# A recommendation model's last tile: layer 4 with features on partitions, an output layer as two products, sums in quarters, and the other tiles' logits stored ahead

## The reference

```
fm = emb_table[arange(26)[None, :], cat_idx]                 # 26 rows of 128
dense = relu(relu(relu(x @ Wd1 + bd1) @ Wd2 + bd2) @ Wdf + bdf)
Z = concatenate([fm, dense[:, None, :]], axis=1)
interactions = einsum('bie,bje->bij', Z, Z)[:, iu, ju]       # 351 pairs
x = concatenate([interactions, dense], axis=-1)
x = relu(x @ Wt1 + bt1); x = relu(x @ Wt2 + bt2)
x = relu(x @ Wt3 + bt3); x = relu(x @ Wt4 + bt4)             # 512 -> 256 in Wt4
return sigmoid(x @ Wo + bo)
```

## Time and profile before

| | us |
|---|---|
| median of 3 runs | 176.47 (176.35 to 177.85) |
| profiled execution | 176.1 |
| its span, first to last instruction | 174.3 |
| TensorE busy | 161.2 (93%) |
| VectorE busy | 72.2 (41%) |
| ScalarE busy | 62.4 (36%) |
| GpSimd busy | 99.9 (57%) |

### The profile page before, as it was taken

The page is one execution under the profiler, slowest core; times in us unless marked ns, Lnnn a source line. Parts: engine busy times, 40 slices in busy tenths (PEclk is TensorE's granted clock), DMA queues, the critical chain, the costliest instruction groups (busy, mean ns, idle before and its releaser), DMA issues.

```text
span 174.3 us, 3885 instructions
## 1 busy us (share of the span) xinstructions
PE 161.2 (93%) x1691; PEld 115.7 (66%) x1691; DVE 72.2 (41%) x139; ACT 62.4 (36%) x108; POOL 99.9 (57%) x111
## 2 busy tenths in 40 slices
PE   2999999589999998899999999999999999999983
PEld 1334464345768785678787867877877777788971
DVE  5005276786664662553504225163212453411311
ACT  3377597848476772031211121311111230201110
POOL 4777777777777777777777777777775000000000
PEclk9999999999999999999999999999999999999999
DMA  2999999329855422121212121211222000000000
GB/s 60 331 385 264 240 315 342 137 58 310 314 171 175 146 56 52 47 64 45 60 49 58 51 56 54 54 52 50 59 49 60 4 0 0 0 4 0 0 0 0
DMA packets 6674, 18.18 MB, mean 104 GB/s; under 512 B 2309, under 2 KB 2441, under 8 KB 6530
## 3 DMA queue, kind: packets, MB, share of 16 engines
q1 hardware_dynamic: 3330, 11.12, 19.6%
q0 software_dynamic: 3328, 6.82, 14.4%
HBM read 17.93 MB, written 0.00 MB: 103 GB/s over the span
## 4 chain that ended last, share of the span: by engine, by line
PE 59%; POOL 21%; issue 8%; DMA 6%; ACT 2%; DVE 1%; DVEq 0%
PE mp L484 23%; POOL rows L345 21%; PE mp L451 8%; PE mp L507 7%; DMA rows<-in_emb,row_of 5%; PE gp L410 4%; PE gp L400 4%; PE tp L459 4%; PE gp L525 3%; PE tp L548 3%; PE mp L548 1%; DMA idx<-in_cat_idx 1%; ACT zt L634 1%; ACT xth L646 1%; ACT a2h L654 1%
## 5 line engine op out<-in xcount | busy, mean ns | idle before, releaser
L345 POOL DMA_INDIRECT rows<-in_emb,row_of x104 | 99.0, 952 | 33.1 <-issue 28.9
L484 PE MATMUL mp<-w2l,a1h 128*128 128x512 f32 x64 | 26.8, 418 | 0.0
L484 PE MATMUL mp<-w2h,a1h 128*128 128x512 f32 x64 | 26.2, 410 | 0.0
L484 PE MATMUL mp<-w2h,a1l 128*128 128x512 f32 x64 | 25.5, 399 | 0.0
L634 ACT COPY zt<-gp 128x512 f32<-128x512 f32 x16 | 9.4, 586 | 31.4 <-PE gp L400 31.3
L400 PE MATMUL gp<-ident,rows 128*128 128x128 f32 x104 | 16.7, 275 | 3.6 <-DMA rows<-in_emb,row_of 3.5
L400 PEld LDWEIGHTS gp<-ident,rows 128*128 128x128 f32 x104 | 12.7, 140 | 10.0 <-DMA rows<-in_emb,row_of 5.8
L410 PEld LDWEIGHTS gp<-zt 128*32 128x32 f32 x1024 | 11.2, 110 | 8.2 <-issue 6.8
L814 DVE TENSOR_TENSOR raw<-mp,bc 128x512 f32<-128x512 f32 x8 | 5.5, 691 | 25.6 <-PE mp L484 25.6
L410 PE MATMUL gp<-zt 128*32 128x27 f32 x1024 | 13.3, 195 | 1.3 <-DVE zt L785 0.8
L484 PEld LDWEIGHTS mp<-w2h,a1l 128*128 128x128 f32 x64 | 12.1, 189 | 2.9 <-DVE a1l L808 0.9
(11 more groups left out here) (85 smaller groups left out, 246.2 us busy)
## 6 DMA issues: line engine op xcount, KB each, us to landing
w<-in_wt SPq DMA_DIRECT2D x13, 512.0 KB, 5.0
rows<-in_emb,row_of POOLq DMA_INDIRECT x104, 2.8
w<-in_wt SPq DMA_DIRECT2D x3, 468.0 KB
bc<-in_rows SPq DMA_DIRECT2D x1, 1024.0 KB, 6.2
wd_sb<-in_wd SPq DMA_DIRECT2D x1, 512.0 KB, 3.5
w1d<-in_wt SPq DMA_DIRECT2D x1, 512.0 KB, 6.1
bt<-in_rows SPq DMA_DIRECT2D x1, 512.0 KB, 8.6
wdf_sb<-in_wdf SPq DMA_DIRECT2D x1, 128.0 KB, 3.3
```

The lines of the kernel that those rows point to most:

```text
L345: pool.indirect_dma_start(out=rows[:, n % RING, :], out_offset=None, in_=emb.rearrange("c v e -> (c v) e"), in_offset=bass.IndirectOffsetO ...
L484: last = pe.matmul(sums_of(t, 2 + h), a[:, k, :], w[:, k, cols], start=(k == 0 and part == 0), stop=(k == M1 - 1 and part == 2))
```

## The change

It touches the fourth tile's last layers and the output.

- The small constants in `sm` get four more columns: the two halves of `bt4` and the two of `Wo`, one value for each partition.
- The second half of layer 3's sum is added in two quarters of 128 columns, each transposed by itself, and each with its own relu. `last_turn` now does one transpose.
- `last_layer_4` takes 128 columns of `w4[:, k]` as the weights in the array and streams `a3[:, k, :]`, for two halves m of the output features: eight products of 128 columns, and the result has output features on partitions, in `mp[:, 0]` and `mp[:, 1]`.
- Bias and relu of half 0 are one instruction of ScalarE, of half 1 one of VectorE, each with a bias per partition, into `a4`.
- The output layer of this tile is two products with a column of `Wo` as the weights (one column wide) and `a4[:, m, :]` streamed; the result is one row of 128 logits.
- The logits of the first three tiles are transposed between layer 2 and layer 3 of the fourth tile, get their sigmoid there, and are stored with a transfer of their own. The fourth tile's row has its own sigmoid and transfer. SP waits for both at the end.

```diff
-for _name, _n in (("bd1", 4), ("bd2", 2), ("bdf", 1), ("bo", 1)):
+for _name, _n in (("bd1", 4), ("bd2", 2), ("bdf", 1), ("bo", 1), ("bt4", 2), ("Wo", 2)):
...
             sp.wait_ge(probs_ready, 1)
-            sp.dma_start(out.rearrange("(t p) c -> t (p c)", p=P), probs[:]).then_inc(out_done, 16)
-            sp.wait_ge(out_done, 16)
+            sp.dma_start(rows_out[0:TILES - 1, :], probs[:]).then_inc(out_done, 16)
+            sp.wait_ge(probs_ready, 2)
+            sp.dma_start(rows_out[TILES - 1:TILES, :], last_probs[:]).then_inc(out_done, 16)
+            sp.wait_ge(out_done, 32)
...
+            def last_turn(t, k):
+
+                pe.wait_ge(raw_ready, TURNS * t + 4 + (1 if k < 2 else k))
+                pe.transpose(last_turned(k, k + 1), raw[:, 0, k * P:(k + 1) * P], ident[:]).then_inc(turned, 1)
...
+            def last_layer_4(t):
+
+                for k in range(M3):
+                    pe.wait_ge(a3_ready, t + (1 if k < 2 else k))
+                    for m in range(2):
+                        last = pe.matmul(mp[:, m, 0:P], w4[:, k, m * P:(m + 1) * P], a3[:, k, :], start=(k == 0), stop=(k == M3 - 1))
+                        if k == M3 - 1:
+                            last.then_inc(l4_ready, 1)
+                        if k < 2 and m == 1 - k:
+                            last_turn(t, 2 + k)
+
+            def turn_logits():
+
+                pe.wait_ge(logits_ready, TILES - 1)
+                pe.transpose(gp[:, 0, 0:P], logits[:], ident[:]).then_inc(logits_turned, 1)
+
+            def last_logits():
+
+                for m in range(2):
+                    pe.wait_ge(a4_act if m == 0 else a4_dve, 1)
+                    last = pe.matmul(gp[0:1, 1, 0:P], sm[:, COLS["Wo"] + m:COLS["Wo"] + m + 1], a4[:, m, :], start=(m == 0), stop=(m == 1))
+                last.then_inc(logits_turned, 1)
...
             layer_1(t)
             layer_2(t)
+            turn_logits()
             last_layer_3(t)
-            layer_4(t)
-            pe.wait_ge(logits_ready, TILES)
-            pe.transpose(mp[:, 0, 0:P], logits[:], ident[:]).then_inc(logits_turned, 1)
+            last_layer_4(t)
+            last_logits()
...
             layer_2_hi(t, 0)
+            sigmoid()
             layer_2_hi(t, 1)
-            for h in range(2):
-                sc.wait_ge(turned, TURNS * t + 4 + h + 1)
-                sc.activation(a3[:, 2 * h:2 * h + 2, :].rearrange("p m b -> p (m b)"), tp[:, h, 0:2 * P], ACT.Relu).then_inc(a3_ready, 1)
-            sigmoid()
+            for k0, k1 in ((0, 2), (2, 3), (3, 4)):
+                sc.wait_ge(turned, TURNS * t + 4 + k1)
+                sc.activation(a3[:, k0:k1, :].rearrange("p m b -> p (m b)"), last_turned(k0, k1), ACT.Relu).then_inc(a3_ready, 1)
+            sc.wait_ge(l4_ready, t + 1)
+            sc.activation(a4[:, 0, :], mp[:, 0, 0:P], ACT.Relu, bias=bias("bt4", 0)).then_inc(a4_act, 1)
+            last_sigmoid()
...
-            for h in range(2):
-                ve.wait_ge(l3_ready, t + h + 1)
-                ve.tensor_tensor(raw[:, 0, 2 * h * P:2 * (h + 1) * P], gp[:, 2 + h, 0:TOP[3] // 2],
-                                 bc[:, ROW3 + 2 * h * P:ROW3 + 2 * (h + 1) * P], ALU.add).then_inc(raw_ready, 1)
-            last_layers(t)
+            for k0, k1 in ((0, 2), (2, 3), (3, 4)):
+                ve.wait_ge(l3_ready, t + k0 // 2 + 1)
+                ve.tensor_tensor(raw[:, 0, k0 * P:k1 * P], gp[:, 2 + k0 // 2, (k0 % 2) * P:((k1 - 1) % 2 + 1) * P],
+                                 bc[:, ROW3 + k0 * P:ROW3 + k1 * P], ALU.add).then_inc(raw_ready, 1)
+            ve.wait_ge(l4_ready, t + 2)
+            ve.tensor_scalar(a4[:, 1, :], mp[:, 1, 0:P], bias("bt4", 1), 0.0, ALU.add, ALU.max).then_inc(a4_dve, 1)
```

More of the change, by code:

```diff
@@ L156, in build @@
         logits = sb("logits", [P, P])
-        probs = sb("probs", [TILES, P])
+        probs = sb("probs", [TILES - 1, P])
+        last_probs = sb("last_probs", [1, P])
+        a4 = sb("a4", [P, 2, P])
         table_warm = sb("table_warm", [P, 1])
@@ L227, in build @@
         a3_ready = sem("a3_ready")
+        a4_act = sem("a4_act")
+        a4_dve = sem("a4_dve")
         l4_ready = sem("l4_ready")
@@ L240, in sums_of, with last_turned @@
             return mp[:, (SUMS * t + i) % 2, :]
-        def layer_4_sums(t):
-            return (tp if t < TILES - 1 else mp)[:, 1, 0:TOP[4]]
+        def last_turned(k0, k1):
+            return tp[:, 1, 0:P] if k0 == 2 else tp[:, 0, (k0 % 3) * P:(k0 % 3 + k1 - k0) * P]
         def pairs_by_chunk(c0, c1):
@@ L323, in _ @@
             sp.dma_start(w4[:].rearrange("p k n -> p (k n)"), wt4).then_inc(w4_in, 16)
+            rows_out = out.rearrange("(t p) c -> t (p c)", p=P)
             sp.wait_ge(probs_ready, 1)
-            sp.dma_start(out.rearrange("(t p) c -> t (p c)", p=P), probs[:]).then_inc(out_done, 16)
-            sp.wait_ge(out_done, 16)
+            sp.dma_start(rows_out[0:TILES - 1, :], probs[:]).then_inc(out_done, 16)
+            sp.wait_ge(probs_ready, 2)
+            sp.dma_start(rows_out[TILES - 1:TILES, :], last_probs[:]).then_inc(out_done, 16)
+            sp.wait_ge(out_done, 32)
         @block.gpsimd
@@ L518, in last_layer_3 @@
                                 last_turn(t, 0)
+                                last_turn(t, 1)
                             k, part = 4 * half + n // 3, n % 3
@@ L541, in layer_4 @@
                 for k in range(M3):
-                    if t < TILES - 1 and k == 0:
+                    if k == 0:
                         pe.wait_ge(a3_ready, t + 1)
[L544 to L548, removed]
-                last.then_inc(l4_ready, 1)
+                    last = pe.matmul(tp[:, 1, 0:TOP[4]], a3[:, k, :], w4[:, k, :], start=(k == 0), stop=(k == M3 - 1))
+                last.then_inc(l4_ready, 1)
+            def last_layer_4(t):
[15 more added lines that the diff above has]
+                last.then_inc(logits_turned, 1)
             def keep_warm(n):
@@ L661, in sigmoid, with last_sigmoid @@
                 sc.wait_ge(logits_turned, 1)
-                sc.activation(probs[:], mp[0:TILES, 0, 0:P], ACT.Sigmoid, bias=sm[0:TILES, COLS["bo"]:COLS["bo"] + 1]).then_inc(probs_ready, 1)
+                sc.activation(probs[:], gp[0:TILES - 1, 0, 0:P], ACT.Sigmoid, bias=sm[0:TILES - 1, COLS["bo"]:COLS["bo"] + 1]).then_inc(probs_ready, 1)
+            def last_sigmoid():
+                sc.wait_ge(logits_turned, 2)
+                sc.activation(last_probs[:], gp[0:1, 1, 0:P], ACT.Sigmoid, bias=sm[0:1, COLS["bo"]:COLS["bo"] + 1]).then_inc(probs_ready, 1)
             sc.wait_ge(ident_made, 2)
@@ L829, in last_layers @@
                 ve.wait_ge(l4_ready, t + 1)
-                ve.tensor_tensor(z4[:, 0, :], layer_4_sums(t), bc[:, ROW4:ROW4 + TOP[4]], ALU.add).then_inc(z4_ready, 1)
+                ve.tensor_tensor(z4[:, 0, :], tp[:, 1, 0:TOP[4]], bc[:, ROW4:ROW4 + TOP[4]], ALU.add).then_inc(z4_ready, 1)
                 ve.wait_ge(z4_ready, t + 1)
```

## The result

| | before | after |
|---|---|---|
| median | 176.66 us (12 runs, 176.30 to 177.85) | 175.37 us (12 runs, 175.09 to 176.14) |
| profiled execution | 176.1 us | 175.6 us |
| its span | 174.3 us | 173.8 us |

The ratio is 0.9926, with a 95% interval of 0.9908 to 0.9944: 1.3 us faster, between 1.0 and 1.6. The forecast was a gain of 1.0 us and a time of 175.5 us.

A forecast was written before the change was run, and what follows sets the result against it. TensorE gapless to 168.15 us, then a 4.56 us chain of short dependent instructions to the store. Its steps, including +0.11 and -0.62 us, moved the store from 172.71 to 171.70: 176.47 - 1.0 = 175.5 us, range 174.9 to 176.5.

The forecast's parts named there:

- relay: Short dependent instructions from the last layer 3 product's end to the last store's issue; 4.56 us before the change.
- Step 1: Three tiles' logits transposed between layers 2 and 3 of the last tile: +0.11 us, with the early sigmoid hidden.
- tail: From the last store's issue to the span's end: taken as unchanged at 1.59 us.
- rival of a much shorter tail: After the last store's issue: most of 0.9 us of waiting vanishes, sum near -1.8 us, 174.7 us; chance 0.05.
- Step 2: Second half of layer 3's sum on VectorE: each quarter 0.29 us instead of 0.42 us for the whole half.
- Step 3: Layer 4 as 16 passes of 128 columns at 0.11 us: ends at 170.38 instead of 171.00, -0.62 us.
- bounds: In layer 4: if waits expose loads at k = 2 or k = 3, up to 0.2 us less gain.
- Steps 4 to 6: Behind layer 4: relus (VectorE 0.40 us, ending last), output products, sigmoid; store at 171.70 instead of 172.71.
- Trainium skill's rule against step 3: In layer 4: weight loads overlap products only in other array rows, so 16 full-height loads would each add to the path.
- step 5: Output layer's second product: 0.34 us plus 0.11 for a second pass, full-width load price kept; at most 0.06 us less.
- The sum: Total over the kernel's end: -1.0 us, bounds -0.8 and -1.2; gain of 0.7 to 1.2 us given chance 0.72.

The follow-up runs named there:

- halves run: Changed kernel with the second half of layer 3's sum added, transposed and relued in one piece again; ratio to the kernel before 0.9970.
- both repetitions: The changed kernel run again unaltered in the first and third rounds against the kernel before; 175.46 and 175.35 us, ratio 0.9922 each time.
- quarters alone: Kernel before with only the second half's sums, transposes and relus in quarters, layer 4 in its old form; ratio to the kernel before 0.9964.

## Why the prediction was right

- *Where the gain lies.* The forecast looked for it in the relay, and there it is: 1.07 us shorter, forecast 1.12 (4.56 to 3.44 from its own figures).
- *Step 1, logits ahead.* The cost of 0.11 us and the full hiding of the early sigmoid were as forecast. The tail, which I kept at 1.59 us, became 0.1 us shorter. The rival of a much shorter tail had the right sign and failed in size: 0.1 us, not most of 0.9.
- *Step 2, sums in quarters.* 0.286 us each for 0.29; the halves run shows what hangs on them, 0.57 us.
- *Step 3, layer 4.* The step was 0.11 us, as I took it from the transposes. Layer 4 ended 2.23 us after layer 3 (169.71 + 1.35 - 168.83); I had 2.12. Of the missing 0.11, 0.07 is a load that shows at k = 2, which I had put in the bounds: the first three of the ten passes from 169.71 end after 0.57 us, where a step of 0.11 would make it 0.50. That load starts at 169.91, 0.05 us after the relu of quarter 2 has ended (169.58 + 0.28). I had let k = 2 go just before TensorE gets there, but its load stands behind the same wait, and the loads here run 0.10 us ahead of their passes when none of them shows (169.61 and 169.71). The other 0.04 is spread over the steps before and after, each a little over 0.11. Three short windows of the changed kernel's timeline (start, us from the first start to the last end, count) show the wait:

```profile
169.71 0.39 PE L558 MATMUL mp<-a,w 128*128 128x128 f32 x2
169.71 0.57 PE L558 MATMUL mp<-a,w 128*128 128x128 f32 x3
169.91 0.41 PEld L558 LDWEIGHTS mp<-a,w 128*128 128x128 f32 x3
```

- *Steps 4 to 6.* From layer 4's end to the store 1.26 us; I had 1.32. VectorE's relu took 0.35 us instead of 0.40. The named order was wrong: I had VectorE's half decide the end. In the trace the four passes of the output layer follow each other by 0.11 us from 171.30, released by ScalarE, and the second product would have had its data at 171.46, before its turn at 171.52. A handoff takes about 0.04 of these 0.06 us, so the two legs are nearly tied. With every product doubled the second half of layer 4 ends 0.44 us behind the first instead of 0.23, and VectorE's relu does stand in the chain. There the second output product follows a wait, as I had it, and its two passes take 0.39 us, where my sum had 0.34 + 0.11 = 0.45:

```profile
173.56 0.39 PE gp L574 x2
```

- *The Trainium skill's rule against step 3.* Full-height loads recorded at 0.19 us stand in steps of 0.11 us between passes, so loads run beside columns here. The rule in "TensorE: Matmul & The Clock Gate" (Trainium skill, Part 3, "The mechanism"), that a load overlaps products only in other rows of the array, does not hold here.
- *The one-column load.* It was recorded at 0.08 us, but it does not show in the passes behind it. The first output pass after the wait took 0.27 us like the other three (270 to 273 ns), where the first pass of layer 4 took 0.377, and four passes cover 0.60 us, where the four at layer 4's start cover 0.71. The formula of the Trainium skill on the same page, section "LDWEIGHTS (loading the stationary operand)", makes a load of one column about 1 ns by estimate; on the path the trace agrees that it costs next to nothing, in the record it does not. The full-width price that I kept in step 5 was too high by 0.06 us (0.39 against 0.45 above), the bound I had named.
- *The sum.* 1.0 us forecast, 1.07 by the trace, 1.3 us (1.0 to 1.6) by the measured times, and 0.78% in both repetitions. That forecast and trace agree so well is in part luck: layer 4 took 0.11 us more than I had, and the stretch behind it 0.06 and the tail 0.11 less. The absolute time had luck too: the kernel before came out at 176.66 us over 12 runs, 0.19 above the 176.47 that I started from, and the larger measured gain made up for it. The trace's figure lies inside all three intervals but below all three middles. What the remaining 0.2 to 0.3 us would be, if real, no run shows: the time up to layer 3's end scatters by more than that, and the kernel before has one profile only. The partial versions show less of it and cannot exclude it: the halves run is 0.53 us faster than before by the measured times (0.2 to 0.9) and 0.46 by its trace (0.50 of relay and 0.07 of tail, less 0.11), the quarters alone 0.64 (0.1 to 1.1) against 0.48.

## What to carry to other kernels

At the end of a kernel, where nothing is left to fill waits, follow the relay from the last gapless instruction to the store: a piece of work cut in two lets the next engine start on the first half while the second is still being made. Here cutting one 256-column sum, with its transposes and relu, in two was worth about as much as a new form of the last two layers. Once one engine follows itself through a stretch, its own work sets the length there: with products doubled nearly every added pass was paid for. Small work from other places can go into the waits that remain. When effects are of 0.1 us and the time up to a fixed point scatters by as much as 1.3 us from profile to profile (layer 3's end: 167.85 to 169.18 us over all kernels here, 168.30 to 168.83 in the three profiles of the changed one), compare lengths between two fixed points inside the trace, not spans.

## What was not expected of the hardware

- Two like VectorE instructions on independent data overlap by 0.09 us (0.61 us for two of 0.35); in the kernel before, the sum and the dot product that needs it had a gap of 0.02 us.
- A bias per partition costs ScalarE 0.09 us (relu of 128 columns 0.367 against 0.277 us; the last sigmoid 0.36 with it, 0.27 without). VectorE's add and maximum with such a bias takes 0.351 us against 0.286 for its sum of two tensors of the same size; the two differ in more than the bias, so its share is not separated.
- A weight load of one column is still recorded at 0.08 us, against 0.19 for 128 columns, but the first pass behind it shows nothing of it (0.27 us, against 0.377 behind a load of 128 columns).
- With a last store of one row behind an earlier one, the tail is about 0.1 us shorter than with a single store of four rows (1.44 to 1.52 us against 1.59 and 1.61). The issue record goes with the rows: 0.29 us for four, 0.28 for three, 0.26 for one.
